# Approach of the late stages to the attention ahead: two steps an item over eight items in place of four steps over four

## The chip, the cores and the metric

The kernel runs on one core of a Trainium2 chip. The metric is the device time of one execution in microseconds (us). TensorE (PE) multiplies matrices, VectorE (DVE) works elementwise and reduces, ScalarE (ACT) evaluates activations and copies, GpSimd (POOL) works elementwise more slowly, and SyncE (SP) issues transfers. Each of them takes its own list of instructions in order and waits for the others through semaphores.

## The reference

A transformer block pair over 16 batches of 256 tokens, width 128, 16 heads of 8. In order: a softmax attention with rotary embedding, a gated feed-forward, a causal attention with sparsemax in place of softmax, and the same feed-forward again, each on a layer norm of x and added to x.

```python
x = x + attn_a(layernorm(x))      # softmax(q k^T / sqrt(8)) v, then Wo
x = x + ffn(layernorm(x))         # (silu(x Wg^T) * (x Wu^T)) Wd^T, hidden 384
x = x + attn_b(layernorm(x))      # sparsemax of causal q k^T / sqrt(8), times v, then w_proj
x = x + ffn(layernorm(x))
```

## The kernel before, in words

The work is cut into 32 items: items 0 to 15 are the first attention and feed-forward of the 16 batches ("soft"), items 16 to 31 the second attention and feed-forward ("plain"). B is 16. An item has 16 heads, and a step is one head: at step 16 n + h TensorE computes head h of item n's first pass of scores (`pass1`, lines 1498 to 1507) and VectorE reduces it (`reduce_head`, for plain items two MAX8, L1115 and L1116). Thirty steps later TensorE computes the same scores again transposed (`pass2`, L1525 to L1531), ScalarE turns them into probabilities (L1307), and every eight steps TensorE multiplies two groups of four heads with v (`pv`, L1544): for plain items at steps that are 0 and 8 modulo 16. I call this a pair of pv.

Everything else of an item is hung on these steps by a table, `AT`, with exceptions for plain items in `PLAIN`: each stage has a number, and the stage of item n is due at step 16 n + number. Every engine's program is one loop over the steps, and in each step it issues the stages that are due, in an order fixed in the code. So the table sets the order of every engine's list, and nothing is moved at run time. All steps below are given modulo 16 where the item is named.

The stages of the table that come after the attention are the late stages, named in `LATE`. For a plain item n they are, with their numbers: `proj` 71 (L1443, output projection on TensorE), `residual`, `f_bn`, `f_aggr` 72 (L1141, L1066, L1072, L1074 on VectorE: adding x and the statistics of the layer norm; together I call them the statistics burst), `fxT` 78 (L1451 on TensorE, ScalarE's copy, and L1148 on VectorE), `gu0`, `gu1`, `gu2` 82, 84, 86 (L1463, L1464 on TensorE: gate and up), `up0` to `up2` 83, 85, 87 (L1156 on VectorE), `hid0` to `hid2` (L986 on GpSimd), `down` 92 (L1472 on TensorE), `f_residual` 92 (L1162 on VectorE) and `store_x` 92 (L861 on SyncE). In a step, VectorE takes the head's reduction first, then `residual` and the statistics, then `tau` (L1124 to L1130, the threshold of sparsemax, at steps 0 modulo 16), and `f_residual` last. `store_x` waits for `f_residual`.

Waits that matter: `pass1` of head h waits until VectorE has reduced head h - 2 (two banks of scores). The dense stages of TensorE (`q`, `v`, `shift`, `xT` of an item ahead, and the late ones) share banks 5, 6 and 7 in turn. SyncE's list holds, for an item ahead, `store_q` (L785, L786; due 15 steps before the item's first head, that is at 1 modulo 16), `store_k` and `load_q` (L793, L802, L805; at 3), `load_shift` (L827; at 7) and `load_k` (L814; at 8). `store_x` comes last within its step. The transfers of q and k go through HBM into `q_stack` and `k_stack`, from which `pass1` of the item reads.

The number of steps by which the late stages come nearer is a function of n in `turn`:

Of the kernel before, what the change touches and what calls it, by code (L numbers as in the profile page):

```python
# [29 lines left out]
B, T, D, H = 16, 256, 128, 16  # L30
# [161 lines left out]
def is_soft(n):  # L192
    return n < B


def wait(eng, s, value):
    if value > 0:
# [17 lines left out]
LATE = ("xb", "proj", "residual", "f_bn", "f_aggr", "f_rstd", "f_norm", "fxT", "gu0", "gu1", "gu2", "up0", "up1", "up2",  # L215
        "hid0", "hid1", "hid2", "down", "f_residual", "store_x")
# [7 lines left out]
def turn(n, what):  # L224

    if n == 1 and what in SECOND:
        return SECOND[what]
    nearer = min(16, 4 * (n - B + 1)) if n >= B and what in LATE else 0  # L230
    at = AT[what] if is_soft(n) else PLAIN.get(what, AT[what])
    return 16 * n + at - nearer


TURNS = {what: {turn(n, what): n for n in range(ITEMS)} for what in AT}


# [402 lines left out]
def main_phase(nc, ctx, m, io):  # L640
# [101 lines left out]
    def wait_filled(eng, use, n):  # L742
        turn, i = place[use, n]
        eng.wait_ge(full[i], turn + 1)

    def wait_freed(eng, use, n):
        turn, i = place[use, n]
        eng.wait_ge(freed[i], turn + 1)
# [954 lines left out]
```

## Time and profile before

| what | value |
|---|---|
| time, median of 3 runs | 602.57 us (601.98 to 603.39) |
| profiled execution | 606.08 us, of it 604.3 us from first to last instruction |
| PE busy / LDWEIGHTS (PEld) busy | 570.3 us (94%) / 438.5 us (73%) |
| DVE / ACT / POOL busy | 485.8 us (80%) / 421.1 us (70%) / 386.3 us (64%) |
| chain that ended last, by engine | PE 65%, DVE 16%, issue 5%, DMA 5%, ACT 4% |

The table is read with the steps beside it: as each item begins with a MAX8 of head 0 on VectorE, the time between two such instructions is the length of an item, and the stretches below are cut there. Item 20 begins at 359.1 us, item 21 at 376.7, 22 at 396.6, 23 at 413.6, 24 at 431.8, 25 at 449.1, 26 at 465.1 and 27 at 481.1 us.

### The profile page before, as it was taken

Reading aid. Unit: us, or ns where it says so; the run is one execution under the profiler, and the core shown is the slowest. Engines: PE = TensorE matmul, PEld = TensorE weight load, DVE = VectorE, ACT = ScalarE, POOL = GpSimd, SP = SyncE. Lnnn points to the kernel's source line nnn. Section 1 sums busy time; section 2 is a strip of 40 time slices with the busy share of each in tenths; the row PEclk is TensorE's granted clock in tenths of the full one; section 3 lists DMA queues with packets and bytes.
Section 4 is the critical chain, followed back from the end, with each engine's and each line's share of the span. In section 5 each row is a group of like instructions: output and inputs, shape, how many; then the busy total and the mean of one; then the engine's idle time right before and its main releaser. Section 6 shows DMA issues by size and latency. Waiting matters only on the chain.

```text
span 604.3 us, 19102 instructions
## 1 busy us (share of the span) xinstructions
PE 570.3 (94%) x6680; PEld 438.5 (73%) x6680; DVE 485.8 (80%) x1426; ACT 421.1 (70%) x1057; POOL 386.3 (64%) x820
## 2 busy tenths in 40 slices
PE   8878999999999999999999999999899999999885
PEld 6655667777776777777677787777788888878664
DVE  3589889889898888988788887798788888898332
ACT  1115668777778777788888777777577778777762
POOL 4755568666767766676777676577576666653342
PEclk9999999999999999999999999999899999999996
DMA  7657765656676765555555544453534455450000
GB/s 216 184 149 164 161 151 154 159 137 152 153 172 148 167 155 138 135 142 149 129 137 140 136 91 109 105 125 80 135 99 121 110 127 119 113 127 13 12 10 22
DMA packets 74656, 76.24 MB, mean 126 GB/s; under 512 B 10348, under 2 KB 68908, under 8 KB 70092
## 3 DMA queue, kind: packets, MB, share of 16 engines
q1 hardware_dynamic: 63636, 68.09, 44.9%
q10 hardware_dynamic: 10920, 6.88, 5.5%
q8 instruction: 55, 0.90, 0.6%
q14 instruction: 45, 0.37, 0.2%
HBM read 46.86 MB, written 23.33 MB: 116 GB/s over the span
## 4 chain that ended last, share of the span: by engine, by line
PE 65%; DVE 16%; issue 5%; DMA 5%; ACT 4%; POOL 2%; SPq 2%; POOLq 0%; ACTq 0%; DVEq 0%
PE banks L1544 14%; PE banks L1498 9%; PE banks L1522 8%; PE banks L1472 6%; PE banks L1411 6%; DVE top L1116 4%; DMA k_stack<-k_image 3%; DVE top L1115 3%; PE banks L1463 3%; DVE neg_shift L1110 2%; PE banks L1464 2%; PE banks L1443 2%; ACT probs_t L1307 2%; PE banks L1501 2%; PE banks L1421 1%
## 5 line engine op out<-in xcount | busy, mean ns | idle before, releaser
L1307 ACT ACTIVATE probs_t<-banks 128x512 f32<-128x512 f32 (+1 forms) x512 | 267.0, 551 | 75.3 <-PE banks L1522 47.3
L1110 DVE TENSOR_REDUCE neg_shift<-banks 128x2 f32<-128x512 f32 x256 | 165.6, 681 | 29.5 <-PE banks L1498 28.1
L1544 PE MATMUL banks<-probs_t,v_ext 128*32 128x256 f32 (+1 forms) x2048 | 118.1, 360 | 0.0
L1116 DVE MAX8 top<-banks 128x8 f32<-128x256 f32 x256 | 106.2, 415 | 0.0
L1498 PE MATMUL banks<-k_stack,q_stack 72*128 72x256 bf16 x512 | 98.9, 274 | 7.7 <-DVE neg_shift L1110 3.6
L1522 PE MATMUL banks<-q_stack,k_stack 75*128 75x256 bf16 x512 | 98.4, 273 | 0.3 <-ACT probs_t L1307 0.2
L986 POOL TENSOR_TENSOR hidden<-up_tanh,gate_half 128x256 f32<-128x256 f32 x96 | 70.0, 731 | 43.6 <-DVE up_tanh L1156 38.1
L1115 DVE MAX8 top<-banks 128x8 f32<-128x128 f32 x256 | 74.3, 290 | 25.2 <-PE banks L1507 24.6
L1544 PEld LDWEIGHTS banks<-probs_t,v_ext 128*32 128x32 f32 x2048 | 55.8, 110 | 39.5 <-issue 13.9
L1498 PEld LDWEIGHTS banks<-k_stack,q_stack 72*128 72x128 bf16 x512 | 39.9, 97 | 47.5 <-DVE neg_shift L1110 36.6
L1463 PE MATMUL banks<-f_xT_high,w_gate_up 128*128 128x256 f32 x192 | 58.5, 326 | 0.9 <-DVE f_xT_low L1148 0.9
L1501 PE MATMUL banks<-mask_b,ident_b 128*128 128x44 bf16 x256 | 47.9, 187 | 9.5 <-DVE top L1116 5.9
L1505 PE MATMUL banks<-k_stack,q_stack 72*128 72x128 bf16 x256 | 56.3, 220 | 0.0
L1507 PE MATMUL banks<-k_stack,q_stack 128*128 128x128 bf16 x256 | 56.3, 220 | 0.0
L1529 PE MATMUL banks<-q_stack,k_stack 75*128 75x128 bf16 x256 | 56.2, 220 | 0.0
L1531 PE MATMUL banks<-q_stack,k_stack 128*128 128x128 bf16 x256 | 56.1, 220 | 0.0
L1503 PE MATMUL banks<-k_stack,q_stack 128*128 128x128 bf16 x256 | 55.4, 216 | 0.0
L1527 PE MATMUL banks<-q_stack,k_stack 128*128 128x128 bf16 x256 | 55.3, 216 | 0.0
L1472 PE MATMUL banks<-wf,hidden 128*128 128x128 f32 x384 | 49.9, 281 | 3.5 <-POOL hidden L986 3.5
L930 POOL TENSOR_TENSOR qk<-rope_cos_terms,rope_sin_terms 128x256 f32<-128x256 f32 x31 | 22.4, 723 | 47.9 <-DVE rope_sin_terms L1089 47.8
L1522 PEld LDWEIGHTS banks<-q_stack,k_stack 75*128 75x128 bf16 x512 | 45.8, 98 | 8.7 <-ACT probs_t L1307 1.0
L918 POOL TENSOR_TENSOR f_rstd<-f_var_eps,neghalf 128x2 f32<-128x2 f32 x32 | 23.0, 718 | 45.5 <-DVE f_var_eps L1074 45.4
(116 smaller groups left out, 1380.6 us busy)
## 6 DMA issues: line engine op xcount, KB each, us to landing
q_stack<-q_image SPq DMA_DIRECT2D x93, 192.0 KB
k_stack<-k_image SPq DMA_DIRECT2D x93, 192.0 KB
q_image<-qk_parts SPq DMA_DIRECT2D x32, 192.0 KB, 2.3
k_image<-qk_parts SPq DMA_DIRECT2D x32, 192.0 KB, 2.1
q_image<-qk_parts SPq DMA_DIRECT2D x32, 128.0 KB, 2.6
o_image<-out_t SPq DMA_DIRECT2D x32, 128.0 KB, 1.9
out_compact<-o_image SPq DMA_DIRECT2D x32, 64.0 KB
rdenominators<-r_image SPq DMA_DIRECT2D x16, 128.0 KB, 3.2
```

The lines of the kernel that those rows point to most:

```text
L986: pool.tensor_tensor(m.hid[:, c, :], m.t1[:, k, :], m.g05[:, k, :], ALU.mult).then_inc(hid_ready, 1)
L1110: dve.tensor_reduce(m.nm[:, n % STACKS, h, :], scores.rearrange("p (q k) -> p q k", q=TT), AX.X, ALU.max, negate=True).then_inc(reduced, 1)
L1115: dve.max(m.z8[:, n % 2, h, 0, :], scores[:, 0:P])
L1116: dve.max(m.z8[:, n % 2, h, 1, :], scores[:, P:P + T]).then_inc(reduced, 1)
L1307: act.activation(m.pt[:, (n * Q + g) % GROUPS, i, 0:size], shifted_banks[:, j % 2, 0:size], ACT.Exp if is_soft(n) else ACT.Relu, scale=SCA ...
L1463: pe.matmul(out, w[:, c * P:(c + 1) * P], m.f_high[:, :], start=True, stop=False)
L1472: ins = pe.matmul(bank("down", n)[:, tt * D:(tt + 1) * D], m.hid[:, c, tt * P:(tt + 1) * P], down_w[:, c * D:(c + 1) * D], start=(c == 0), ...
L1498: ins = pe.matmul(scores[:, qt * T:(qt + 1) * T], qs[0:STACK, h, qt * P:(qt + 1) * P], ks[0:STACK, h, :], start=True, stop=True)
L1501: pe.matmul(blocks(scores, REST), m.ident_b[:, :], twice(m.mask_b, REST), start=True, stop=True, skip_group_check=True)
L1505: pe.matmul(scores[:, P:T], qs[0:STACK, h, P:T], ks[0:STACK, h, 0:P], start=False, stop=True, skip_group_check=True)
L1522: ins = pe.matmul(shifted[:, kt * T:(kt + 1) * T], ks[0:SHIFTED, j, kt * P:(kt + 1) * P], qs[0:SHIFTED, j, :], start=True, stop=True)
L1544: ins = pe.matmul(out_bank[32 * i:32 * i + 32, at + skip:at + T], v_windows(v, kt)[:, Q * g + i, :], m.pt[:, (n * Q + g) % GROUPS, i, kt * ...
```

## The change

`nearer` grows by 2 steps an item in place of 4, up to the same 16. For items 16, 17, 18, 19, 20, 21, 22 and 23 it was 4, 8, 12, 16, 16, 16, 16, 16 and is 2, 4, 6, 8, 10, 12, 14, 16. So the late stages of items 16 to 22 come 2, 4, 6, 8, 6, 4 and 2 steps later than before, and those of all other items stay where they were. The late stages of neighbouring items are 14 steps apart over eight items, where they were 12 apart over four. No instruction is added or taken away.

```diff
     if n == 1 and what in SECOND:
         return SECOND[what]
-    nearer = min(16, 4 * (n - B + 1)) if n >= B and what in LATE else 0
+    nearer = min(16, 2 * (n - B + 1)) if n >= B and what in LATE else 0
     at = AT[what] if is_soft(n) else PLAIN.get(what, AT[what])
     return 16 * n + at - nearer
```

The first place is VectorE's list around step 324 (item 20, head 4). L1141 to L1074 are the statistics burst of item 16, L1059 and L1061 the statistics of the attention ahead, L1156 an `up`. Before:

```order
L1115 MAX top<-banks 128x8
L1116 MAX top<-banks 128x8
L1141 TENSOR_TENSOR x<-banks,x_plus_bias 128x256
L1066 BN_STATS f_bn_out<-x 128x6 x2
L1072 BN_AGGR f_mean_var<-f_bn_out 128x2 x2
L1074 TENSOR_SCALAR f_var_eps<-f_mean_var 128x2
L1059 BN_AGGR a_mean_var<-a_bn_out 128x2 x2
L1061 TENSOR_SCALAR a_var_eps<-a_mean_var 128x2
L1156 SCALAR_TENSOR_TENSOR up_tanh<-gate_tanh,banks 128x256
```

Now, from the same L1156 on:

```order
L1156 SCALAR_TENSOR_TENSOR up_tanh<-gate_tanh,banks 128x256
L1115 MAX top<-banks 128x8
L1116 MAX top<-banks 128x8
L1115 MAX top<-banks 128x8
L1116 MAX top<-banks 128x8
L1141 TENSOR_TENSOR x<-banks,x_plus_bias 128x256
L1066 BN_STATS f_bn_out<-x 128x6 x2
L1072 BN_AGGR f_mean_var<-f_bn_out 128x2 x2
L1074 TENSOR_SCALAR f_var_eps<-f_mean_var 128x2
L1115 MAX top<-banks 128x8
L1116 MAX top<-banks 128x8
L1156 SCALAR_TENSOR_TENSOR up_tanh<-gate_tanh,banks 128x256
```

The burst of item 16 stands two heads later, at step 326.

The second place is TensorE's list in step 416 (item 26, head 0). L1501 to L1507 are `pass1`, L1421 `v` of item 27, L1525 to L1531 `pass2`, L1544 the first rows of the pair of pv. Before:

```order
L1501 MATMUL banks<-mask_b,ident_b 128x2x22
L1503 MATMUL banks<-k_stack,q_stack 128x128
L1505 MATMUL banks<-k_stack,q_stack 128x128
L1507 MATMUL banks<-k_stack,q_stack 128x128
L1421 MATMUL banks<-wb,a_xT 128x128 x2
L1525 MATMUL banks<-maskT_b,ident_b 128x2x22
L1527 MATMUL banks<-q_stack,k_stack 128x128
L1529 MATMUL banks<-q_stack,k_stack 128x128
L1531 MATMUL banks<-q_stack,k_stack 128x128
L1544 MATMUL banks<-probs_t,v_ext 32x256 x4
```

Now:

```order
L1507 MATMUL banks<-k_stack,q_stack 128x128
L1421 MATMUL banks<-wb,a_xT 128x128 x2
L1451 MATMUL banks<-cc,f_xhat 128x128 x2
L1472 MATMUL banks<-wf,hidden 128x128 x6
L1525 MATMUL banks<-maskT_b,ident_b 128x2x22
L1527 MATMUL banks<-q_stack,k_stack 128x128
L1529 MATMUL banks<-q_stack,k_stack 128x128
L1531 MATMUL banks<-q_stack,k_stack 128x128
L1544 MATMUL banks<-probs_t,v_ext 32x256 x4
```

The step has taken in `fxT` of item 22 and `down` of item 21. They stood two and four steps earlier, at 414 and 412.

The third place is SyncE's list, where `store_x` (L861) stands among the transfers of the item ahead. `q_stack1` and `k_stack1` belong to item 25 here, `q_stack2` to item 26. One piece of the difference:

```order
 L805 DMA q_stack1<-zero_rows 3x16x256
-L827 DMA q_stack3<-neg_shift_rows 3x16x256
-L814 DMA k_stack1<-k_image 24x4096 x3
-L861 DMA out_0<-x2 128x2x128
-L785 DMA q_image<-qk_parts 128x3x256
-L786 DMA q_image<-qk_parts 128x2x256
+L861 DMA out_0<-x2 128x2x128
+L827 DMA q_stack3<-neg_shift_rows 3x16x256
+L814 DMA k_stack1<-k_image 24x4096 x3
+L785 DMA q_image<-qk_parts 128x3x256
+L786 DMA q_image<-qk_parts 128x2x256
+L861 DMA out_0<-x2 128x2x128
```

Behind it follow L793 and L802 of item 26 in both. `store_x` of item 19 has moved from behind the load of k for item 25 to the place ahead of it, at step 388, and `store_x` of item 20 now stands at step 402, between the store of q and the store of k for item 26. Over the whole list, `store_x` of items 16 to 23 was due at 8, 4, 0, 12, 12, 12, 12, 12 modulo 16 and is due at 10, 8, 6, 4, 2, 0, 14, 12.

## Rows read from the trace of the kernel before

**Rows 1.** The page: the span, and the busy time of each engine.

```profile
span 604.3 us, 19102 instructions
PE 570.3 (94%) x6680; PEld 438.5 (73%) x6680; DVE 485.8 (80%) x1426; ACT 421.1 (70%) x1057; POOL 386.3 (64%) x820
```

**Rows 2.** Busy time by stretch: items 20 to 26, then 21, 23, 24, 25, 26.

```profile
core 0: us, PE busy (x) PEld busy (x) DVE busy (x) ACT busy (x) POOL busy (x), PEclk, DMA share, GB/s
...
359.10:481.10 122.00, 114.83 (x1668) 97.00 (x1668) 103.07 (x369) 89.58 (x247) 81.55 (x175) 0.99 0.44 109
...
376.70:396.60 19.90, 17.51 (x248) 14.46 (x247) 16.36 (x61) 14.54 (x41) 12.49 (x27) 1.00 0.41 104
...
413.60:431.80 18.20, 16.49 (x245) 14.22 (x244) 14.93 (x54) 12.22 (x34) 12.51 (x28) 1.00 0.56 131
431.80:449.10 17.30, 17.22 (x239) 14.15 (x239) 13.94 (x52) 12.22 (x34) 9.94 (x22) 0.90 0.37 93
449.10:465.10 16.00, 15.68 (x239) 13.31 (x237) 14.31 (x53) 12.39 (x34) 11.26 (x25) 1.00 0.48 121
465.10:481.10 16.00, 15.64 (x237) 13.21 (x235) 14.26 (x52) 12.39 (x34) 11.13 (x25) 1.00 0.45 120
```

**Rows 3.** Timeline: start, us; the waits of TensorE at two statistics bursts.

```profile
363.80 0.41 DVE L1141 TENSOR_TENSOR x<-banks,x_plus_bias 128x256 f32<-128x256 f32 x1
...
366.73 0.20 PE L1501 MATMUL banks<-mask_b,ident_b 128*128 128x44 bf16 x1 [1.42 <-DVE top L1116]
...
394.78 0.19 PE L1501 MATMUL banks<-mask_b,ident_b 128*128 128x44 bf16 x1 [0.99 <-DVE top L1116]
```

**Rows 4.** Timeline in item 26: a statistics burst and the pair of pv.

```profile
473.28 0.41 DVE L1141 TENSOR_TENSOR x<-banks,x_plus_bias 128x256 f32<-128x256 f32 x1
...
474.78 0.30 DVE L1115 MAX8 top<-banks 128x8 f32<-128x128 f32 x1
...
472.80 1.51 PE L1544 MATMUL banks<-probs_t,v_ext 128*32 128x256 f32 x32
```

**Rows 5.** Timeline of VectorE in item 21, behind `down` and pv.

```profile
388.35 0.30 DVE L1115 MAX8 top<-banks 128x8 f32<-128x128 f32 x1 [1.51 <-PE banks L1507]
```

**Rows 6.** The chain that ended last, in order of time: start, us, what.

```profile
416.04 0.34 DVE x L1162
416.39 0.42 SPq L861
416.91 0.41 SPq L785
417.37 2.15 DMA q_image<-qk_parts
419.53 0.31 SPq L802
...
423.20 7.84 DMA k_stack<-k_image
...
432.20 2.72 PE banks L1544 x32
...
441.00 1.44 PE banks L1544 x32
```

**Rows 7.** TensorE's wait in the timeline, and the stretch after it.

```profile
431.14 0.18 PE L1501 MATMUL banks<-mask_b,ident_b 128*128 128x44 bf16 x1 [1.57 <-DMA k_stack<-k_image]
...
433.00:435.00 2.00, 2.00 (x31) 1.12 (x24) 0.71 (x2) 0.02 (x1) 0.97 (x5) 0.50 0.90 252
```

**Rows 8.** Timeline of SyncE around the start of item 25.

```profile
447.06 0.42 SPq L861 DMA_DIRECT2D out<-x  x1
448.19 0.38 SPq L785 DMA_DIRECT2D q_image<-qk_parts  x1
...
451.21 1.68 SPq L802 DMA_DIRECT2D q_stack<-q_image  x3
...
456.16 1.19 SPq L814 DMA_DIRECT2D k_stack<-k_image  x3
```

## The prediction

> **What bounds the kernel now.** I read the page first, then the busy times by stretch, then the chain that ended last, and last the timeline at its longest stops. The page shows no engine free enough to forget and none full: TensorE busy 94% of the span, VectorE 80% [rows 1]. Such a share is an average over stretches with different lengths, so I cut the span at the start of each item. Items 25 and 26 take 16.0 us each, and they are the regular beat of the plain items [rows 2]. Items 20 to 26 together take 122.0 us [rows 2], where seven regular ones would take 7 x 16.0 = 112.0 us. These 10.0 us over the beat are where the change acts: the late stages of items 16 to 22 run there, and the lists outside it are the same. Part of the 10.0 us cannot go away in either kernel, because the late stages come 16 steps nearer, and so one item's late stages more than the beat has are done in the stretch.
>
> The regular beat is an arrangement in which long pieces lie side by side. In item 26 VectorE's statistics burst begins at 473.28 and the next MAX8 at 474.78, so that the burst and the reduction are 1.50 us apart, and TensorE's pair of pv runs beside it from 472.80 for 1.51 us [rows 4]. Neither engine waits for the other. In item 20 the burst is at step 4 of 16, where no pair of pv stands, and TensorE waits 1.42 us for the MAX8 behind it; in item 21 the burst of item 18 is at step 12, and TensorE waits 0.99 us [rows 3]. The longest item is 21, with 19.9 us [rows 2]: there `down` of item 16 falls on a pair of pv, and this time VectorE stands still, for 1.51 us [rows 5].
>
> The chain shows a third kind of loss, which no busy share shows. `f_residual` of item 18 ends at 416.38, only then SyncE issues `store_x` (416.39), and only then the stores and loads for item 24, which stand behind it: L785 at 416.91, the first load of q at 419.53, and k is in place at 423.20 + 7.84 = 431.04 [rows 6]. TensorE has waited 1.57 us for it, and the granted clock behind the wait is 0.50, which is 1.2 GHz of 2.4 [rows 7]. The pair of pv that runs there takes 2.72 us where it takes 1.44 at the full clock [rows 6], a loss of 1.28 us. On the beat the same list runs without this: `store_x` is out at 447.06, before q is ready at 448.19 [rows 8].
>
> **The change part by part.** Nothing is added or removed, so the sum has only terms for where things fall.
>
> *Statistics bursts off their cover.* The burst is due at 72 - `nearer`. Before, items 16, 17, 18 had it at 4, 0, 12 modulo 16 and from 19 on at 8. Now items 16 to 22 have it at 6, 4, 2, 0, 14, 12, 10, and item 23 at 8. A pair of pv stands at 0 and 8. Bursts without a pair beside them: two before (4 and 12), six now. The two seen cost TensorE 1.42 and 0.99 us, 1.2 on average [rows 3]. Not all of it is net: the pair of pv at step 8 that has lost its burst is shorter for the step, and TensorE works off a little of it later. The trace does not show the net. Its bounds are 0 (all given back) and 1.42 us. I take 0.8, nearer to the rows seen than to nothing, since TensorE has little idle time to give back in this stretch. Four more bursts: +3.2 us, with bounds 0 and +5.7.
>
> *Less crowding.* Before, the late stages of four items begin within 36 steps of each other, now those of eight within 98. The worst meeting before is `down` on a pair of pv, at steps 8 (item 16) and 0 (item 18) modulo 16; now it happens twice as well, for item 17 at 8 and for item 21 at 0, and the latter has `fxT` of item 22 in the same step. But between them more steps are quiet, so a stop is followed by room to catch up. I take back 1.1 us, some three quarters of the one stop of 1.51 us [rows 5]. The bounds are 0, and item 21 falling to the mean of its neighbours: items 20, 22 to 26 take 122.0 - 19.9 = 102.1 us, or 17.0 each, which is 2.9 less than 19.9 [rows 2].
>
> *SyncE's list.* Of every moved `store_x` I ask what stands behind it. At 10, 8 and 14 (items 16, 17, 22) the next entry is not ready earlier or waits little. At 6 and 4 (items 18 and 19) `load_shift` and `load_k` stand behind; the case at 4 exists before (item 17) and made no stop of TensorE. At 0 (item 21) it is the case of the rows: from the release of `store_x` to k in place 431.04 - 416.39 = 14.65 us, the release 2.8 us after the item's start at 413.6 [rows 2, 6], so k is in place 17.5 us after the start; one L1148 more stands ahead of the release now, 17.9. In the rows TensorE begins the next item at 431.14, 0.7 us before its first MAX8 at 431.8 [rows 2, 7]. So it wants k at some 17.0 if item 26 takes 17.7 us (16.0, the one `down` of 1.4 that it gains, and some wait). A stop of 0.9 us before item 27. At 2 (item 20) the release comes about 5 us into item 25; the store of k and then the loads of q stand behind it, which start at 5.9; from the first load of q to k in place the rows have 431.04 - 419.53 = 11.51 us [rows 6], so 17.4, against 16.0 wanted if item 25 takes 16.7. A stop of 1.4 us before item 26. The stop before item 24 goes away, for `store_x` at step 368 is now at 374, behind the load of q. Sum: 0.9 + 1.4 - 1.57 = +0.7 us, with one stretch at the lower clock before and one now. Bounds: no stop and no lower clock, 0 - 1.57 - 1.28 = -2.9 us; two stops as long as the old one, both with the lower clock, +2.9 us.
>
> The clock is a place where a page of the Trainium skill can be held against a row. The trace has the granted clock at 0.50 right behind a wait of 1.57 us [rows 7]. The Trainium skill ("TensorE: Matmul & The Clock Gate", "Why this matters for your kernels") ties such drops to longer idle gaps than this one. By the page the stretch at the lower clock would not be owed to this wait and would stay as it is in both kernels, which leaves the term at +0.7 us. By the row each stop brings 1.28 us, and with two of them the term is +2.0 us.
>
> *Sum.* 3.2 - 1.1 + 0.7 = +2.8 us. The profiled execution is 604.3 us long between first and last instruction, 606.08 as timed, so 1.8 us lie around it; the changed kernel's would be 607.1 and 608.9. That execution is 3.5 us above the median of the runs. On the median of 602.57 us the sum gives 605.4 us. A measurement of this kernel tells about 0.2% (1.2 us) from no change.
>
> **The rivals.** *Crowding was the whole loss (faster).* Item 21 falls to 17.0 us, -2.9, and the uncovered bursts are absorbed because TensorE has more quiet steps around them; SyncE's term is about nothing. That gives 599.7 us, and it decides as soon as four more bursts cost less than about 2.1 us together, 0.5 each. For it: VectorE is only 16.36 of 19.9 us busy in item 21, so the item is long from meetings and not from work. Against it: at step 4 and at step 12 TensorE waited over 0.9 us each, and the one at step 4 came before the crowd. A measure from the rows points the same way as this rival: weight loads are busy 26.52 of 32.0 us on the beat, 83%, and 97.00 of 122.0 us in items 20 to 26 [rows 2]; at 83% throughout these would take 117.0 us, so 5.0 us is the most that any order could win here, and 597.6 us the floor. The Trainium skill ("Perfetto Trace Analysis", "Identifying the Most-Contended Engine") names this share, and not the matmuls' busy time, as the measure of TensorE's headroom. I give the rival 21%.
>
> *A wash.* The bursts cost 0.5 each (2.0), crowding gives back 2.9, SyncE costs 0.7: 602.4 us. Both kernels do the same work over the same 122 us, and small waits may be swallowed by the two banks of scores. 20%.
>
> *Two stops with two stretches at the lower clock (much slower).* The bursts and crowding as in my sum, and SyncE's term at its upper end: 3.2 - 1.1 + 2.9 = +5.0, 607.6 us. For it speaks that the one stop seen brought the lower clock; against it that the waits of 1.42 and 0.99 us in items 20 and 21 did not, as the clock in item 21 is 1.00 [rows 2]. 14%.
>
> **How the numbers follow.** My forecast, moderately slower, 45%: 605.4 us, its own range 603.8 to 607. With the two-stop case slower by over 0.2% has 59%, within 0.2% 20%, faster 21%. The range reaches down to the faster rival at 600.0 and up past the two-stop case to 608.5, and leaves out about a tenth on either side.
>
> **What would show it.** Items 20 to 26 would add up to about 125 us in place of 122.0, with item 21 near 17.5 and items 22, 23 and 26 each above 17.5. Waits of TensorE for L1116 of about 1 us would stand at steps 6, 4, 2, 14, 12 and 10 of items 20 to 25. `store_x` would be issued just ahead of L793 about 5 us into item 25 and just ahead of L785 about 3 us into item 26, and TensorE would wait for `k_stack` at the starts of items 26 and 27, and no longer at item 24; the half clock would follow one of these. If no wait of TensorE over 0.7 us is to be seen at the bursts, the largest term is wrong and the faster rival holds. If k is in place without a wait at 26 and 27, the SyncE term is wrong, and the result lies near 602 us. Before item 20 and from item 28 on the traces should agree to 0.2 us.

## The result: 3% slower, and the profile after

| | before | after |
|---|---|---|
| median of the runs, us | 602.98 (601.98 to 604.8, 4 runs) | 621.33 (619.12 to 624.87, 4 runs) |
| profiled execution: span, us | 604.3 | 619.3 |
| items 20 to 26, us | 122.00 | 137.94 |

The ratio is 1.029, with a 95% interval of 1.0237 to 1.0351. The prediction said 605.4 us and 608.5 at most. The direction was right, and the size was wrong by some 16 us.

The page of the changed kernel answers to [rows 1]:

```profile
span 619.3 us, 19102 instructions
PE 576.9 (93%) x6680; PEld 442.4 (71%) x6680; DVE 487.6 (79%) x1426; ACT 422.4 (68%) x1057; POOL 385.9 (62%) x820
```

The same instructions, and the same busy time of VectorE and ScalarE to 2 us. TensorE is busy 6.6 us longer. The time was lost in waits, so the busy shares don't show where. The stretches, cut at the first MAX8 of each item, do. They answer to [rows 2]; the first is items 20 to 26, and then each item by itself up to 27:

```profile
core 0: us, PE busy (x) PEld busy (x) DVE busy (x) ACT busy (x) POOL busy (x), PEclk, DMA share, GB/s
360.17:498.11 137.94, 121.21 (x1665) 101.61 (x1665) 105.43 (x370) 91.05 (x247) 82.77 (x178) 0.95 0.40 96
360.17:377.01 16.84, 15.70 (x231) 13.04 (x231) 14.30 (x52) 12.73 (x34) 11.26 (x25) 1.00 0.42 103
377.01:396.61 19.60, 16.89 (x245) 14.19 (x243) 14.78 (x54) 13.16 (x36) 11.05 (x25) 1.00 0.37 91
396.61:417.12 20.51, 16.92 (x241) 13.77 (x240) 14.63 (x53) 13.16 (x36) 11.16 (x25) 1.00 0.38 94
417.12:439.70 22.58, 20.64 (x276) 17.26 (x275) 16.92 (x59) 13.80 (x38) 12.97 (x28) 0.85 0.38 99
439.70:459.45 19.75, 15.78 (x210) 13.70 (x200) 15.37 (x52) 12.21 (x33) 11.25 (x24) 0.91 0.37 98
459.45:477.30 17.85, 16.13 (x236) 13.22 (x235) 14.38 (x52) 13.45 (x36) 11.18 (x27) 1.00 0.41 89
477.30:498.11 20.81, 19.16 (x251) 16.43 (x250) 15.05 (x55) 12.54 (x35) 13.90 (x30) 0.92 0.45 99
498.11:514.02 15.91, 15.72 (x240) 13.45 (x239) 14.11 (x53) 12.23 (x34) 9.44 (x22) 1.00 0.48 121
```

The stretch grew by 15.94 us and the span by 15.0, so the loss lies here: item 20 begins at 360.17 us where it began at 359.10, and item 27 has the beat of 15.9 us. Before, only item 21 took over 19 us. Now five of the seven take 19.6 us or more. Three of them have a mean clock below full.

Where an item loses shows when it is cut at each head's second MAX8. Three steps take 5.6, 4.5 and 5.6 us, where most take about one; the longest of before took 3.9 us. They are step 8 of item 22, step 6 of item 23 and step 0 of item 26. Step 0 of item 23 follows with 4.3 us, where it took 3.4 before. Timeline of VectorE and TensorE in the first of them (start, us, engine, line; in brackets the idle time before the instruction and what ended it):

```profile
405.64 0.41 DVE L1116 MAX8 top<-banks 128x8 f32<-128x256 f32 x1
...
409.03 0.42 DVE L1148 TENSOR_TENSOR f_xT_low<-banks,f_xT_high 128x256 fp32r<-128x256 f32 x1 [2.97 <-ACT f_xT_high L1325]
409.37 0.41 DVE L1162 TENSOR_TENSOR x<-banks,x 128x256 f32<-128x256 f32 x1
411.03 0.30 DVE L1115 MAX8 top<-banks 128x8 f32<-128x128 f32 x1 [1.25 <-PE banks L1507]
...
407.28 0.44 PE L1451 MATMUL banks<-cc,f_xhat 128*128 128x128 f32 x2 [1.89 <-ACT f_xhat L1277]
407.55 1.50 PE L1472 MATMUL banks<-wf,hidden 128*128 128x128 f32 x12
409.18 1.51 PE L1544 MATMUL banks<-probs_t,v_ext 128*32 128x256 f32 x32
```

`fxT` of item 18, `down` of item 17 and the pair of pv stand in one step. TensorE first waits 1.89 us for the normalized x, and then has 3 us of dense work ahead of it, during which VectorE gets no scores. The reason for the first wait is the norm. It runs from VectorE's statistics over GpSimd and ScalarE to TensorE, and its timeline is this:

```profile
401.61 0.17 DVE L1074 TENSOR_SCALAR f_var_eps<-f_mean_var 128x2 f32<-128x2 f32 x1
...
403.09 0.72 POOL L986 TENSOR_TENSOR hidden<-up_tanh,gate_half 128x256 f32<-128x256 f32 x1 [1.52 <-DVE up_tanh L1156]
403.98 0.72 POOL L910 TENSOR_TENSOR a_rstd<-a_var_eps,neghalf 128x2 f32<-128x2 f32 x1 [0.17 <-DVE a_var_eps L1061]
405.13 0.71 POOL L918 TENSOR_TENSOR f_rstd<-f_var_eps,neghalf 128x2 f32<-128x2 f32 x1
...
406.35 0.88 ACT L1277 ACTIVATE f_xhat<-x,f_norm_bias,f_rstd 128x128 f32<-128x128 f32 x2 [1.80 <-POOL f_norm_bias L921]
```

The variance is there at 401.78. GpSimd takes it up at 405.13, 3.35 us later, since `hidden` of the item ahead and the norm of the attention ahead (L910 to L913) stand in front of it, and `hidden` waits 1.52 us for VectorE's `up_tanh`. For items 16 to 23 this delay is 1.6, 3.0, 3.4, 3.5, 2.9, 1.6, 1.6 and 2.1 us. In the kernel before it was 2.4 us for item 16 and 0.08 us for each of the others. The list of waits (in total, times, longest) has this wait of ScalarE at 11.1 us where it was 3.7, and VectorE's wait behind it at 8.7 us where it was 3.5:

```profile
DVE f_xT_low L1148 <- ACT f_xT_high L1325: 8.7, 9, 3.0
...
ACT f_xhat L1277 <- POOL f_norm_bias L921: 11.1, 8, 3.2
```

The waits of TensorE for the MAX8, the answer to [rows 3], and its wait for k, the answer to [rows 7]:

```profile
385.33 0.19 PE L1501 MATMUL banks<-mask_b,ident_b 128*128 128x44 bf16 x1 [1.22 <-DVE top L1116]
...
421.86 0.20 PE L1501 MATMUL banks<-mask_b,ident_b 128*128 128x44 bf16 x1 [1.47 <-DVE top L1116]
...
443.00 0.22 PE L1501 MATMUL banks<-mask_b,ident_b 128*128 128x44 bf16 x1 [2.12 <-DVE top L1116]
...
476.69 0.18 PE L1501 MATMUL banks<-mask_b,ident_b 128*128 128x44 bf16 x1 [1.24 <-DMA k_stack<-k_image]
...
497.49 0.18 PE L1501 MATMUL banks<-mask_b,ident_b 128*128 128x44 bf16 x1 [0.73 <-issue]
```

Only the first of these stands where the prediction wanted it (burst of item 17, step 4 of item 21). The second stands behind the burst of item 19 and `tau`, which now share step 0 of item 23: VectorE works from the burst to the end of `tau` without a MAX8 between. The third stands behind `tau` alone. Of the other bursts only the one at step 12 of item 24 brings a wait of this kind, 0.99 us; those at 6 (item 20), 2 (item 22), 14 (item 23) and 10 (item 25) bring none over 0.3 us. For the last line above the profile names no releaser. It is a wait for k all the same: the last packet of k for item 27 landed at 497.40, 0.09 us ahead of the instruction, as the one for item 26 did at 476.60, 0.09 us ahead of 476.69. Three stretches at a clock of 0.50 (1.2 GHz), one of 6.83 us and two of 3.41, begin at 422.54, 443.02 and 477.16: behind the wait of 1.47, that of 2.12, and that of 1.24 us for k. They are 13.65 us in the stretch; before, it was one of 3.41 us. Windows of 2 us across the first one's start and across the third:

```profile
421.00:423.00 2.00, 0.85 (x12) 0.68 (x13) 2.00 (x9) 0.78 (x2) 0.80 (x2) 0.89 0.90 234
423.00:425.00 2.00, 1.87 (x19) 1.34 (x16) 1.97 (x11) 0.90 (x4) 1.77 (x6) 0.50 0.31 70
...
478.00:480.00 2.00, 2.00 (x12) 2.00 (x11) 1.52 (x4) 0.38 (x1) 1.78 (x4) 0.50 0.00 0
```

SyncE did what the prediction read from its list. Timeline of SyncE, the answer to [rows 8]:

```profile
464.09 0.39 SPq L861 DMA_DIRECT2D out<-x  x1
464.58 0.41 SPq L793 DMA_DIRECT2D k_image<-qk_parts  x1
465.09 1.24 SPq L802 DMA_DIRECT2D q_stack<-q_image  x3
...
481.23 0.42 SPq L861 DMA_DIRECT2D out<-x  x1
482.10 0.39 SPq L785 DMA_DIRECT2D q_image<-qk_parts  x1
```

`store_x` goes out 4.6 us into item 25 and 3.9 us into item 26 (predicted: 5 and 3), and k comes late for both items behind, by 1.24 and 0.73 us (predicted: 1.4 and 0.9). One stretch at the lower clock followed, as predicted. So the smallest term was read well, and the loss is elsewhere.

### The profile page after: what moved, and what is told of

Its sections match the earlier page's. It is cut to its first block, busy times and chain, and to the rows that moved or that the text cites. A ratio compares the mean times of both kernels' runs of the same rounds, so it can differ in the third digit from the quotient of the medians.

```text
span 619.3 us, 19102 instructions
## 1 busy us (share of the span) xinstructions
PE 576.9 (93%) x6680; PEld 442.4 (71%) x6680; DVE 487.6 (79%) x1426; ACT 422.4 (68%) x1057; POOL 385.9 (62%) x820
## 4 chain that ended last, share of the span: by engine, by line
PE 65%; DVE 14%; issue 7%; POOL 6%; ACT 4%; DMA 2%; SPq 1%; POOLq 0%; ACTq 0%; DVEq 0%
PE banks L1544 14%; PE banks L1498 8%; PE banks L1522 8%; PE banks L1472 8%; PE banks L1411 6%; DVE top L1116 4%; PE banks L1463 2%; PE banks L1464 2%; DVE top L1115 2%; DVE neg_shift L1110 2%; PE banks L1501 2%; ACT probs_t L1307 2%; PE banks L1443 2%; PE banks L1421 2%; PE banks L1503 1%
## 5 line engine op out<-in xcount | busy, mean ns | idle before, releaser
L1544 PE MATMUL banks<-probs_t,v_ext 128*32 128x256 f32 (+1 forms) x2048 | 117.7, 359 | 0.0
L1544 PEld LDWEIGHTS banks<-probs_t,v_ext 128*32 128x32 f32 x2048 | 55.5, 109 | 39.4 <-issue 13.5
L1501 PE MATMUL banks<-mask_b,ident_b 128*128 128x44 bf16 x256 | 48.1, 188 | 11.7 <-DVE top L1116 8.8
L1507 PE MATMUL banks<-k_stack,q_stack 128*128 128x128 bf16 x256 | 56.7, 222 | 0.0
L1531 PE MATMUL banks<-q_stack,k_stack 128*128 128x128 bf16 x256 | 56.5, 221 | 0.0
L1472 PE MATMUL banks<-wf,hidden 128*128 128x128 f32 x384 | 52.8, 291 | 3.7 <-POOL hidden L986 3.7
L1472 PEld LDWEIGHTS banks<-wf,hidden 128*128 128x128 f32 x384 | 50.7, 206 | 4.9 <-POOL hidden L986 4.1
L1525 PE MATMUL banks<-maskT_b,ident_b 128*128 128x44 bf16 x256 | 48.1, 188 | 6.3 <-ACT probs_t L1307 5.9
```

The costliest lines, as they stand in the source:

```text
L1472: ins = pe.matmul(bank("down", n)[:, tt * D:(tt + 1) * D], m.hid[:, c, tt * P:(tt + 1) * P], down_w[:, c * D:(c + 1) * D], start=(c == 0), ...
L1501: pe.matmul(blocks(scores, REST), m.ident_b[:, :], twice(m.mask_b, REST), start=True, stop=True, skip_group_check=True)
L1544: ins = pe.matmul(out_bank[32 * i:32 * i + 32, at + skip:at + T], v_windows(v, kt)[:, Q * g + i, :], m.pt[:, (n * Q + g) % GROUPS, i, kt * ...
```

## The experiments

All edits are to `turn` or to what it returns, so every kernel has the instructions of the changed one in another order, and nothing of the computation is left out. "The stretch" is items 20 to 26 of the profiled execution: 122.00 us before, 137.94 after. Where a whole time has a ratio, it is to runs of the kernel before on the same chip. Edits are to the changed kernel if nothing else is said. e6, e7, e12, e13 and e14 were run once each.

**Is it the meeting of `fxT` and `down`?** `fxT` has number 78 and `down` 92. With neighbours 14 steps apart, `fxT` of one item is due in the very step of `down` of the item ahead (78 + 16 - 2 = 92), seven times over. Two edits part them by a step, one by the later `down`, one by the later `fxT`:

```diff
+MOVED = dict(down=1, f_residual=1, store_x=1)     # e1; in e2: dict(fxT=1)
...
+    if B <= n < B + 7:
+        at += MOVED.get(what, 0)
     return 16 * n + at - nearer
```

> The changed kernel with down, f_residual and store_x of items 16 to 22 due one step later, so that fxT of the next item and down no longer share a step (fxT keeps its step, down is the step behind). Theory A (the late stages of neighbouring items, 14 steps apart, put fxT and down into one step, and the meeting itself costs): seven such meetings are undone, and of the 16 us that items 20 to 26 grew by (122.0 to 137.9) 5 to 8 come back: 613 to 616 us. Theory B (fxT comes late because its layer norm goes through GpSimd's list behind hidden and a_rstd, and TensorE and VectorE stop for it): fxT keeps its step and its lateness, so nothing or at most 2 us comes back: 619 to 622 us.

Measured: 622.54 us, ratio 1.031 [1.0232, 1.0388], the stretch 138.98 us.

> The changed kernel with fxT (TensorE's transposes, ScalarE's copy, VectorE's low part) of items 16 to 22 due one step later, behind down and no longer in its step. Theory A (the meeting in one step costs): as when down is moved, 5 to 8 us come back, 613 to 616 us. Theory B (the norm is late): each fxT gets one step of 0.5 to 2 us more for its norm, and down fills TensorE meanwhile, so 4 to 8 us come back as well, 613 to 617 us. Against the kernel with down moved it tells: only A expects the two to be alike.

Measured: 621.5 us, ratio 1.0304 [1.0234, 1.0375], the stretch 137.21 us. Neither moved the time, so theory A falls: sharing the step is not the cause. The clearer case is e2, which has 13.65 us at the lower clock in the stretch, as the changed kernel has, and its three long steps of 4.4, 4.5 and 5.4 us. e1 has 20.48 us at the lower clock, which may hide up to 3.4 us of gain. In it step 8 of item 22 takes 6.1 us, and the other two places at most 3.4. Theory B had expected 4 to 8 us from e2 as well, and this fell too: `fxT` one step later is not enough.

**Is it the late norm?** GpSimd's part of the norm is issued two steps sooner and ScalarE's one, so that it stands ahead of the `hidden` that waits:

```diff
+MOVED = dict(f_rstd=-2, f_norm=-1)     # and as above, for items 16 to 22
```

> The changed kernel with f_rstd (GpSimd) of items 16 to 22 due two steps sooner and f_norm (ScalarE) one step sooner, so that the layer norm stands ahead of hidden and a_rstd in GpSimd's list; TensorE's and VectorE's lists stay word for word. In the trace of the changed kernel f_rstd of item 18 begins at 405.13 us although VectorE's statistics were done near 402, and TensorE then stops 1.89 us for f_xhat and VectorE 2.97 us for the copy. Theory B (late norm): the stops before fxT of items 18, 19, 21 and 22 shrink, 6 to 12 us come back with the clock that follows them, 609 to 615 us. Theory A (meeting of fxT and down in a step): 619 to 622 us, since the lists of TensorE and VectorE are unchanged.

Measured: 616.16 us, ratio 1.0208 [1.0141, 1.0275], where the changed kernel has 1.029 [1.0237, 1.0351]. The four runs take 615.40 to 617.11 us, where those of the changed kernel take 619.12 to 624.87. 609 to 615 us had been expected, a little more than came. The window of items 20 to 26:

```profile
360.35:491.30 130.95, 117.47 (x1665) 97.57 (x1665) 104.56 (x369) 90.92 (x247) 82.14 (x177) 0.99 0.41 101
```

It is 6.99 us less. The timeline at the same place as above (lines stand 5 further down here, and `f_rstd` is L923):

```profile
401.46 0.72 POOL L923 TENSOR_TENSOR f_rstd<-f_var_eps,neghalf 128x2 f32<-128x2 f32 x1 [2.56 <-DVE f_var_eps L1079]
...
404.13 0.28 PE L1435 MATMUL banks<-ident_b,neg_shift_parts 128*128 128x128 bf16 x2 [0.54 <-POOL neg_shift_parts L962]
405.05 0.39 PE L1456 MATMUL banks<-cc,f_xhat 128*128 128x128 f32 x2
...
408.32 0.42 DVE L1153 TENSOR_TENSOR f_xT_low<-banks,f_xT_high 128x256 fp32r<-128x256 f32 x1 [2.31 <-ACT f_xT_high L1330]
```

TensorE no longer waits for the norm, and the three long steps take 3.9, 3.4 and 4.0 us in place of 5.6, 4.5 and 5.6, which is 4.4 us of the 7. Only one stretch at the lower clock is left in the window, 3.41 us in place of 13.65, and this gives back the remainder or part of it. Items 21 and 22, which are at the full clock in both traces, are 0.6 and 1.4 us shorter, so 2.0 of the 7 us are waits alone. How the other 5.0 divide can't be told: the clock fell behind the waits.

**SyncE.** `store_x` of items 16 to 21 goes to step 12 modulo 16, where it has no load behind it that is due:

```diff
-    return 16 * n + at - nearer
+    due_at = 16 * n + at - nearer
+    if what == "store_x" and B <= n < B + 6:
+        due_at += (12 - due_at) % 16
+    return due_at
```

> The changed kernel with store_x of items 16 to 21 moved back in SyncE's list to the next step that is 12 modulo 16, where it stands on the regular beat, so that no load waits behind it. My prediction's third term: the waits for k before items 26 and 27 (1.24 and 0.73 us in the trace) and the 3.41 us at the lower clock behind the first of them go, 2 to 4 us come back, 617 to 619 us. Rival: k is late for another reason (split on GpSimd late) or the waits are only moved, under 1 us comes back, 620 to 622 us.

Measured: 620.34 us, ratio 1.028 [1.0208, 1.0351], the stretch 135.86 us, 2.1 less. The whole time is in the range of the rival (620 to 622 us) and not told from the changed kernel's. The trace shows where the gain went. TensorE waits for k nowhere in the stretch, and items 25 and 26 are 1.2 and 2.0 us shorter, but the clock fell in item 21, where it had not in the changed kernel, and that item is 1.0 us longer. The same was tried on the kernel before, where the one store that stops k is item 18's:

```diff
     nearer = min(16, 4 * (n - B + 1)) if n >= B and what in LATE else 0
+    if what == "store_x" and n == B + 2:
+        nearer -= 4
```

> The kernel before with one transfer moved: store_x of item 18 four steps later in SyncE's list (from 368 to 372), so that the store of q and k and the load of q for item 24 no longer stand behind it. My reading of the chain (k is 1.57 us late for item 24 because of it, and the pair of pv behind runs at the lower clock, 1.28 us more): 2 to 3 us faster than before, 600 us. Rival (the wait is taken up by the next one): within 0.7 us of before.

Measured: 602.51 us over 10 runs, ratio 0.9988 [0.9958, 1.0018]; the window of items 20 to 26:

```profile
359.11:478.34 119.23, 113.35 (x1668) 96.21 (x1668) 102.68 (x370) 89.78 (x247) 81.69 (x175) 1.00 0.44 112
```

2.77 us less, and the prediction's reading was 1.57 + 1.28 = 2.85 us for the wait and for the clock behind it. In the whole time no difference is told from none, and the interval reaches down to -2.5 us only. The trace of before had the clock fall behind this stop; other executions of it need not have it. One of them ran at a mean clock of 0.999 of the full one, and a single such fall of 3.41 us would have left 0.997. So the clock's share of the 2.77 us is not shown for every execution.

Both mends of the changed kernel together:

> The changed kernel with both edits that gave something: f_rstd two steps and f_norm one step sooner for items 16 to 22, and store_x of items 16 to 21 in the slot of the beat. The first alone gave 616.2 us against 621.3, the second 620.3. If they add up: 613 to 615 us, items 20 to 26 in 128 to 130 us. If store_x's slot only mattered through the lower clock, which the first edit has already mostly removed: 615.5 to 616.5 us.

Measured: 616.47 us, ratio 1.0203 [1.0144, 1.0262], the stretch 131.24 us: as with the sooner norm alone. The two don't add up. The trace has 6.83 us at the lower clock in the stretch where e3 has 3.41, which may hide up to 1.7 us; whether a stop at one place also covers one at another was not measured.

**How many items stand off the beat, and where?** The next kernels change only the approach itself. Eight items in pairs (4, 4, 8, 8, 12, 12, 16, 16):

```diff
-    nearer = min(16, 2 * (n - B + 1)) if n >= B and what in LATE else 0
+    nearer = min(16, 4 * ((n - B) // 2 + 1)) if n >= B and what in LATE else 0
```

> Nearer by 4, 4, 8, 8, 12, 12, 16, 16 steps for items 16 to 23: the approach takes eight items as in the change, but neighbours are 16 or 12 steps apart, never 14, and only the three offsets of the kernel before (4, 8, 12) occur, each twice. Theory C (what costs is being off the beat, by so much an item whatever the spacing): six or seven off-beat items in place of three, 608 to 614 us. Theory D (the offsets 2, 6, 10, 14 and the spacing of 14 cost, not the length of the approach): 601 to 606 us.

Measured: 613.75 us, ratio 1.0193 [1.013, 1.0256], the stretch 129.82 us. The theory that each item off the beat costs holds (608 to 614 us), and D falls (601 to 606). The kernel before has offsets 4, 8 and 12 once each and this one twice each, both have one stop for k and one stretch of 3.41 us at the lower clock, and the three more items cost 129.82 - 122.00 = 7.8 us.

The two ends of the scale, two items (`min(16, 8 * (n - B + 1))`) and no approach at all (`nearer = 0`):

> Nearer by 8 steps an item over two items (8, 16), the other side of the change: one off-beat item in place of three. In the kernels that hold an offset the middle items are 17.3 us long at 2, 18.3 to 20.0 at 4, 18.9 at 6, 17.9 at 8, 18.4 at 10 and 17.5 at 12, against 15.9 at 16. Theory C (each item off the beat costs what its offset costs): without the items at 4 and 12 items 20 to 26 lose 2.4 to 4 and 1.6 us, and store_x of item 18 no longer stands ahead of the loads for item 24 (2.8 us, in place of it store_x of item 17 at 12): 596 to 600 us. Rival (crowding: two sets of late stages within 8 steps collide): the stretch stays at 122 us or grows, 602 to 608 us.

> No approach at all (nearer is 0 for every item): every plain item is on the beat, also over items 20 to 26, and the late stages of the last item end 16 steps later. Theory C: items 20 to 26 take 7 x 15.9 = 111.5 to 113 us, 9 to 10 us less than before, and the end behind the last head takes one item's late stages and the wait between, 8 to 12 us more: 600 to 606 us in all. Rival (the stretch is slow because of the passage from soft to plain items, not because of the offset): items 20 to 26 stay over 118 us, and the whole is 608 us or more.

Measured: e9 602.9 us over 10 runs, ratio 0.9984 [0.995, 1.0018]; e10 605.65 us, ratio 1.0012 [0.9984, 1.004]. The windows of items 20 to 26, of e9 first:

```profile
360.61:479.49 118.88, 113.45 (x1670) 96.08 (x1669) 103.34 (x369) 90.03 (x248) 80.71 (x173) 1.00 0.44 112
```

```profile
362.71:475.17 112.46, 109.81 (x1638) 92.67 (x1638) 99.56 (x359) 86.83 (x238) 78.36 (x167) 1.00 0.48 117
```

For e9 theory C had expected a stretch 6.8 to 8.4 us shorter than before's and 596 to 600 us in all. It is 3.1 us shorter, and the whole time is in the rival's range: items 20 and 21 take 21.2 and 17.9 us, and only then comes the beat. So a change by 8 steps costs more than the offset it stops at. e10 came out as expected. With no approach the stretch is seven beats of 16.07 us, and what follows item 27's start is 131.95 us long where it was 123.18. The 8.8 us at the end are what the approach is there to save. Of the 6.4 us between the two windows some 3.6 are work that belongs to the approach (TensorE 113.45 and 109.81 us busy), the rest is the cost of the two items of the passage.

**An item held at one offset.** The late stages of four plain items in turn stay at the same `nearer`, at 4, 8, 12, and at 2, 6, 10 (`4 * ((n - B) // 4 + 1)`, and `4 * ((n - B) // 4) + 2`):

> Each offset held for four items (4, 8, 12, 16 steps), neighbours 16 steps apart within a group: the length of an item in the middle of a group is the beat at that offset, without any extra late stages in it. The beat at 16 is 15.9 us. My prediction's first term (0.8 us for a statistics burst without a pair of pv beside it) expects 16.7 us at 4 and 12 and 15.9 to 16.2 at 8. Theory C expects 17 to 18 us at each, Theory D 16.0 to 16.5 us. The whole time is longer than that of the kernel before by the later end, and is not compared.

> The same with 2, 6, 10 and 14 steps held for four items each. My prediction's first term expects 16.7 us at all four. Theory C: 17 to 18 us at all four. Theory D (these offsets cost because GpSimd's list puts hidden and a_rstd ahead of the layer norm there): over 18 us at 6 and 8-like offsets where the norm comes late, near 16.5 us at the others. The whole time is not compared.

Measured, the lengths of whole items with the offset held, against 15.9 to 16.1 us on the beat: 17.3 at 2; 18.3 at 4 (20.0 and 19.9 where the clock fell); 18.9 at 6 (19.2 where it fell); 17.9 at 8; 17.4 at 10; 18.6 at 12. Item 28 is left out in both kernels, 18.4 us in e7 and 17.5 in e6: it holds `down` of item 23 still at the offset before. (The expectation of e9 has these two among its lengths.) All pass the first term's 16.7 us and theory D's 16.5, and those at 4, 6 and 12 also theory C's 18. Offset 14 is not measured. Windows of one item each, of e6 at 4, 8 and 12:

```profile
395.89:414.16 18.27, 15.85 (x237) 13.24 (x235) 14.67 (x52) 12.65 (x35) 10.94 (x25) 1.00 0.50 106
...
470.70:488.55 17.85, 15.74 (x237) 13.24 (x236) 15.10 (x53) 12.43 (x35) 11.30 (x25) 1.00 0.44 108
...
527.16:545.73 18.57, 16.09 (x237) 13.25 (x236) 14.71 (x52) 12.73 (x35) 11.17 (x25) 1.00 0.46 103
```

And of e7 at 2, at 6, and in the item between, in which the offset goes from 2 to 6:

```profile
396.25:413.55 17.30, 16.06 (x237) 13.22 (x236) 14.36 (x53) 12.61 (x34) 11.03 (x25) 1.00 0.48 112
430.85:454.60 23.75, 20.59 (x249) 16.53 (x247) 15.25 (x54) 13.64 (x38) 11.25 (x25) 0.86 0.32 82
...
473.81:492.75 18.94, 16.27 (x237) 13.20 (x235) 14.69 (x52) 12.39 (x34) 11.04 (x26) 1.00 0.40 102
```

In all of these windows but the one between offsets TensorE is busy 15.7 to 16.3 us, about as on the beat. An item off the beat costs 1.3 to 3 us by its position alone, at the full clock. At 4 two meetings are part of it, which the timeline of TensorE in item 22 and of VectorE behind it shows: TensorE waits for the MAX8 behind the burst, and VectorE for TensorE behind `down` and the pair of pv.

```profile
403.76 0.19 PE L1501 MATMUL banks<-mask_b,ident_b 128*128 128x44 bf16 x1 [1.61 <-DVE top L1116]
...
408.03 0.30 DVE L1115 MAX8 top<-banks 128x8 f32<-128x128 f32 x1 [1.51 <-PE banks L1507]
```

The same with the sooner norm tells whether the norm is part of this cost (`MOVED` of e3, for all items from 16 on):

> The kernel that holds 2, 6, 10 and 14 steps for four items each, with f_rstd two steps and f_norm one step sooner for all plain items. At 6, where the late norm shows (f_xhat 1.0 us late for TensorE, the copy 1.95 us late for VectorE), the item length falls from 18.9 us to 17 or 17.5; at 2 (17.3 us), where no such stop is in the trace, it stays within 0.3 us. If instead the statistics burst and down make up all of the offset's cost, 6 stays over 18.5 us. The whole time is not compared.

Measured: 17.30 us at 2, 18.71 at 6, 17.48 at 10, so at most 0.2 us is gained while an offset is held, and the expectation fell. The edit did what it should: at 6, GpSimd takes up the norm 3.0 us after its variance in e7 and 0.08 us after it in e12. So in a settled order at 6 the norm is late too, but it costs next to nothing there. Where the offset goes from 2 to 6 it does cost; this item takes 19.16 us in place of 23.75, at the full clock in place of 0.86:

```profile
427.60:446.76 19.16, 17.46 (x249) 14.68 (x247) 15.29 (x54) 13.56 (x38) 11.35 (x25) 1.00 0.43 101
```

Where it goes from 6 to 10, in item 28, nothing is gained (18.66 us, and 18.42 without the edit). A late norm can thus cost much while the offset changes, but not at every change. Why it costs at one place and not at another was not taken apart.

**The two meetings by themselves, on the beat.** With `nearer = 0`, the statistics burst two steps sooner (off the pair of pv) together with `proj` and `xb` (GpSimd's x_plus_bias) ahead of it, or `down` four steps later (onto it):

```diff
+MOVED = dict(xb=-2, proj=-2, residual=-2, f_bn=-2, f_aggr=-2)     # e13
+MOVED = dict(down=4, f_residual=4, store_x=8)                     # e14
```

> No approach, every plain item on the beat, but xb, proj, residual and the statistics two steps sooner (burst at 6 modulo 16, no pair of pv beside it, everything else of the late stages in its place). An item is 15.9 us long with the burst at 8. My prediction's first term: 16.7 us. If the burst alone makes up the cost of the offset of 2 (17.3 us), where it stands at 6 as well: 17.2 to 17.4 us. If TensorE gives it all back: 15.9 to 16.1 us.

> No approach, every plain item on the beat, but down and f_residual four steps later (at 0 modulo 16, on a pair of pv and tau) and store_x eight steps later (at 4, so that SyncE's list has no load behind it). If down on a pair of pv is what the offsets 4, 8 and 12 pay for: 16.7 us or more an item, against 15.9. If only the burst costs: 15.9 to 16.2 us. In the kernel before, the two such meetings went with a stop of VectorE of 1.51 us and with the longest item.

Windows of one item: e10, e13 and e14.

```profile
427.35:443.29 15.94, 15.62 (x238) 13.24 (x235) 14.25 (x53) 12.39 (x34) 11.21 (x25) 1.00 0.50 122
```

```profile
443.04:459.88 16.84, 15.76 (x238) 13.26 (x235) 14.36 (x52) 12.46 (x34) 11.14 (x25) 1.00 0.46 114
```

```profile
441.00:457.73 16.73, 15.77 (x236) 13.23 (x235) 13.98 (x52) 12.12 (x34) 11.28 (x25) 1.00 0.46 115
```

A burst off its cover at step 6, with `proj` and `xb` moved along, costs 0.9 us net, and `down` on a pair of pv and `tau` 0.8. The 0.9 us don't stand in e13 as a wait of TensorE for the MAX8 behind the burst: there is none over 0.3 us there. In its place TensorE waits 0.66 us for VectorE's `up_tanh` and 0.39 us for ScalarE's probabilities, and VectorE 0.81 us for scores. Held at 4, both meetings fall together, and they make up 1.7 of its 2.3 us. Held at 8, neither is there (the burst has a pair of pv beside it, at step 0, and `down` is at 4), and still 1.9 us are lost.

**A shorter approach than before's.** If the cost goes by items off the beat, two items should do better than four. The kernel of e9 once more, and with the sooner norm for item 16:

> The approach in two items (8, 16) with f_rstd two steps and f_norm one step sooner for item 16 alone. In the trace of the two-item approach item 20 is 21.2 us long, and TensorE waits there 0.32 and 0.76 us for f_xhat and 0.66 us for VectorE's low part. If the late norm is behind these: items 20 to 26 fall from 118.9 to 117 to 118 us, and the whole is 1 us below the two-item approach. If crowding is: no difference over 0.5 us.

> The approach in two items again, unchanged, for a narrower interval. Its stretch of items 20 to 26 was 118.9 us against 122.0 before, so 2 to 3 us faster in the whole if nothing else moves, a ratio of 0.995 to 0.997. If the gain of the stretch is lost in the run's own spread, the ratio is 0.998 to 1.002.

Measured: e15 603.0 us over 12 runs, ratio 0.9973 [0.994, 1.0005], the stretch 118.52 us; e16 603.17 us over 12 runs, ratio 0.9971 [0.9946, 0.9997], the stretch 118.86 us. The approach in two items is faster than the kernel before by about 0.3%, at the edge of what can be told. The sooner norm adds nothing that can be seen there, and it had nothing to take away: GpSimd takes up the norm 0.08 us after its variance in e9 already. Nor is the approach in two items told from the one in four with `store_x` of item 18 moved: the stretch of e8 is 119.23 us long.

## Why the prediction was wrong, step by step

**Bursts off their cover (+3.2, bounds 0 to +5.7): the size was right.** 0.8 us was taken for each and 0.9 measured (e13, at step 6 alone), so four more would be +3.6 us. That each would show as a wait of 1 us at its own step was wrong: only those at 4 and 12 do, and the one at 0 meets `tau`. So the price fits better than the reason given for it.

**Less crowding (-1.1, bounds 0 to -2.9): this is the step that failed,** and by its sign. It held one stop of 1.51 us for the whole price of late stages that lie off their place, and took the quiet steps between as room to catch up. Its upper bound was 0, so that no loss of this kind was in the range. The runs showed two things instead. The second of them is a cost that the prediction put at nothing without a reason.

First, an item off the beat costs 1.3 to 3 us each time (e6, e7). Before had three of them (4, 8, 12), after has seven. From the held items at the full clock I work out 2.3 + 1.9 + 2.6 = 6.8 us for 4, 8, 12 (over a beat of 16.0); e4, which has these three once more than before, has a stretch 7.8 us longer. For 2, 4, ..., 12 it is 1.3 + 2.3 + 2.9 + 1.9 + 1.4 + 2.6 = 12.4, and with an estimate of 2 for offset 14, from 10 and 12, 14.4. That is 7.6 us more, of which the bursts are 3.6, so 4.0 us are outside of the term for them. `down` on a pair of pv is not in the difference, as it happens twice in both.

Second, the norm of items 16 to 22 comes 1.6 to 3.5 us late behind GpSimd's list, where before only that of item 16 did. Issuing it sooner gave back 7.0 us of the stretch (e3), the clock included. The prediction worked out what is queued behind a moved step for SyncE alone, and not for GpSimd, though the norm's one hard wait is there.

**SyncE's list (+0.7, bounds -2.9 to +2.9): read rightly, and its two sides measured.** The stop of before was worth 2.8 us in the stretch (e8), those of after 2.1 (e5), which is -0.7 us. By items 25 and 26 alone, without the fall of the clock in item 21, those of after were 3.3, which is +0.5.

**The sum.** 7.6 + 7.0 - 0.7 = 13.9 of the 15.9 us, or 15.1 with +0.5 for SyncE. The parts are rough: e11 shows that the mends don't add, and against the stretch of e10 the same prices overshoot. For before, 6.8 + 2.8 + 3.6 of work make 13.2 us where the windows differ by 122.0 - 112.5 = 9.5; for after, 14.4 + 7.0 + 2.1 + 3.6 make 27.1 where they differ by 25.4. So an item that only passes through an offset seems to pay somewhat less than one held there, before above all, and something of the difference is left without a name. The terms of norm and clock are one number here. TensorE ran 10.24 us more at the lower clock in the stretch, which is worth 5.1 us at most (at half speed, if it was never waited for otherwise). Why an item held at an offset is longer was taken apart only in part: at 4 and 12 the burst and `down` are some of it, while the 2.9 us at 6 and the 1.9 at 8 stay open.

**The rivals.** That crowding was the whole loss is refuted: with more room between the meetings the items got longer. Its measure, weight loads busy 83% of the time on the beat, pointed to a gain of up to 5.0 us. The Trainium skill ("Perfetto Trace Analysis", "Identifying the Most-Contended Engine") names this share, beside the share of peak arithmetic, as the measure of TensorE's headroom. Here it is the distance to the beat and says nothing on whether an order comes nearer to it: weight loads are busy 101.61 of 137.94 us, 74%, in the slower kernel. The prediction let the rival decide once four more bursts cost less than 2.1 us together; that leaves -0.8 us, within the 1.2 us that it calls no change, so the bound should have been 1.7. The rival of two stops at the lower clock had the right mechanism at a wrong place: two of the three stretches came behind waits for VectorE. Held against the rows, the Trainium skill ("TensorE: Matmul & The Clock Gate", "Why this matters for your kernels") ties such drops to longer gaps; here they stand right behind waits of 1.24 to 2.12 us, and not behind every such wait (below).

**What the rows of before could have told.** The 10.0 us over the beat, less the 2.85 of the stop for k, are 2.4 us for each of the three items off the beat, and four more at this price are +9.5 us. e9 and e10 show that this is too simple, since 3.6 us of it are work that doesn't repeat, and with them taken out it is 1.2 us each and +4.7. But it has the right sign, and the prediction instead put the stops that it could name against a gain.

## What to carry to other kernels

A steady order of stages is worth more than its parts show: every item held at another offset pays 1 to 3 us here, although no engine has more to do. So a shift of stages made gently over many items is dear: eight took 137.94 us of stretch, or 129.82 in pairs, and four took 122.00. Going on from four to two gains little: 118.9 us against the 119.23 of four without the stop for k. When stages move against each other, follow every engine's list for what now stands behind a wait, GpSimd's small steps of a norm too. And of a term that is meant to be a gain, the other sign belongs into the bounds unless a row excludes it.

## What the runs showed of the hardware that had not been expected

The granted clock fell to 0.50 behind waits of TensorE of 1.57 us in the kernel before [rows 7] and 1.47, 2.12 and 1.24 us in the changed one. It did not fall behind waits of 1.89 us (item 22) and 1.22 us (item 21) in the changed kernel, nor behind 1.42 us before [rows 3]. So the length of the last wait alone does not decide it. Nor does TensorE's work decide it: e5 has TensorE's and VectorE's lists of the changed kernel and the same wait in item 21, 1.23 us, and there the clock did fall (at 386.28). What decides was not settled. Within items 20 to 26 the stretches were 3.41 us long, or 6.83, twice as much.

Kernels with the same lists up to item 20 begin it between 358.2 and 362.7 us, and runs of one kernel differ too (619.12 to 624.87 us for the changed one). In its profiled execution 1.1 us come with an early stretch at the lower clock, at 53.9 us. So the comparisons here rest on the stretch of one execution each, and the parts of it that hang on the clock are those of that execution.
